# First attention: VectorE normalises an older group before, not after, the sixth row maximum of a pass

## The chip, the cores and the metric

The kernel runs on one core of a Trainium2 chip. The metric is the device time of one execution, in microseconds (us). The engines are named as in the profile: PE is TensorE (matmuls), PEld its loading of weights, DVE is VectorE, ACT is ScalarE, POOL is GpSimd and SP is SyncE, which issues the DMAs here. All run at once, each works through its own instructions in order, and they meet at semaphores.

## The reference

An input x of 4 sequences, 512 tokens each, 128 features, goes through two residual blocks. The change touches only the first, a causal attention of 16 heads with 8 features each:

```python
q = _gelu(apply_rope(x @ wqr + bqr));  k = _gelu(apply_rope(x @ wkr + bkr))
v = _gelu(x @ wkv + bkv) @ wv + bv
scores = einsum('bhqd,bhkd->bhqk', q, k) / sqrt(8), causal
attn = softmax(scores);  out = einsum('bhqk,bhkd->bhqd', attn, v) @ wo + bo
x = x + layernorm(that of layernorm(x));  x = x + layernorm(six layers of local attention and FFN)
```

The second block is six layers of windowed attention and gated FFN, and takes most of the time. Nothing of it is changed.

## The kernel before

**The first attention.** The 16 heads of each of the 4 sequences are cut into 4 groups of 4 heads, which gives 16 groups (`GROUPS`). A group goes through three passes of a software pipeline, so that pass i works on three groups at once: it finds the row maxima of group i, computes the exponentials of group i-1, and divides the outputs of group i-2 by their sums. Passes 0 to 17 run; each has 8 steps n = 0 to 7 (`A_STEPS`).

**One step.** PE scores two heads of group i, queries by keys (`score_for_max`, matmuls of L888), then scores two heads of group i-1 again, keys by queries with the maximum already subtracted (`score_for_exp`, L906), and then adds the causal mask to the first of these (`cut_later_keys`, L895). DVE takes the negated row maxima of the first (L676), ACT the exponentials of the second (L535), and POOL clears the masked corner (L480). The widths fall over the steps: 512 keys in steps 0 and 1, 128 in steps 6 and 7.

**What a pass has besides.** After step 4 (`OUT_AFTER`), PE turns the summed outputs of group i-2 into rows of tokens (`turn_out`, L934), and DVE's `normalise(i-2)` takes the reciprocal of the 16 sums of each token (L664) and multiplies (L666, into a_o, which lies in k_hat). DVE does that in step 5, behind that step's row maximum. At the end of a pass PE multiplies the exponentials with the values (`mix_heads`, L917), and between its parts turns the row maxima (`turn_max`, L926); DVE adds them to the queries (L682), and ACT copies the outputs (L540).

**The ring of PSUM slots.** All these results go through four PSUM slots (`a_ring`, two banks each), used in turn in the order of `a_plan`: in each step max, exp; after step 4 out; after step 7 turn. A user of a slot waits until the one four places earlier has been read (`wait_slot`). Around step 5 the order is: exp 3, max 4, exp 4, **out**, max 5, exp 5, max 6, **exp 6**, max 7, exp 7, turn. So exp 6 takes the slot of out and waits for `a_onorm`, which the multiply of `normalise` raises; max 7 takes the slot of max 5 and waits for its row maxima (`a_max`); the mixing and turn take the slot of max 6.

```python
                elif kind == "out":
                    pe.wait_ge(a_onorm.sem, a_onorm.done(group))
```

PE's own order in a step is fixed: max n, exp n, cut n; behind step 4 also `turn_out`. The heads' queries and keys come to their padded places by SP's DMAs (`move_heads(b)`, L393), those of sequences 2 and 3 after the last exponential scores of sequences 0 and 1.

Of the kernel before, what the change touches and what calls it, by code (L numbers as in the profile page):

```python
# [17 lines left out]
A_GROUPS, A_STEPS, A_ROW, OUT_AFTER = 4, 8, 9, 4  # L18
# [103 lines left out]
def sandwich_kernel(nc, x, wqr, bqr, wkv, bkv, wkr, bkr, wv, bv, wo, bo, w_qk, w_vt, w_o, qk_scale, w1, w2, ffn_vec,  # L122
                    c_ident, c_rope, c_causal, c_ones, c_band, c_sel, c_sel_rows, c_rot, out):
    ctx = ExitStack()
    with ctx:
# [221 lines left out]
        def ring(kind, group, n):  # L347

            at = a_plan.index((kind, group, n))
            return a_ring[at % len(a_ring)], a_plan[at - len(a_ring)] if at >= len(a_ring) else None  # L350

        def max_step(n):

            return TT - 1 - n // 2, n % 2
# [261 lines left out]
        def _(vector):  # L616
# [42 lines left out]
            def normalise(group):  # L659
                b, g = group // A_GROUPS, group % A_GROUPS  # L660
                slot, _ = ring("out", group, OUT_AFTER)
                o = slot[:, 0, :].rearrange("p (t j n) -> p t j n", t=TT, j=4)
                dve.wait_ge(a_oturned.sem, a_oturned.done(group))
                nc.vector.reciprocal(a_inv[:, :, :], o[:, :, :, A_HD]).then_inc(a_recip.sem, 1)  # L664
                dve.wait_ge(a_recip.sem, a_recip.done(group))
                nc.vector.tensor_tensor(a_o[:, b, :].rearrange("p (t j g d) -> p t j g d", t=TT, j=4, g=A_GROUPS)[:, :, :, g, :], o[:, :, :, 0:A_HD],  # L666
                                        a_inv[:, :, :].unsqueeze(3).to_broadcast([P, TT, 4, A_HD]), ALU.mult).then_inc(a_onorm.sem, 1)

            for i in range(GROUPS + 2):
                for n in range(A_STEPS):  # L670
                    if i < GROUPS:
                        qt, pair = max_step(n)
                        slot, _ = ring("max", i, n)
                        top_row = a_nmax[:, qt, :].rearrange("p (j n) -> p j n", j=4)[:, 2 * pair:2 * pair + 2, A_HD]
                        dve.wait_ge(a_scored.sem, a_scored.done(i, n))
                        nc.vector.tensor_reduce(top_row, slot[:, :, 0:P * (qt + 1)], AX.X, ALU.max, negate=True).then_inc(a_max.sem, 1)  # L676
                    if n == OUT_AFTER + 1 and i >= 2:
                        normalise(i - 2)
                if i < GROUPS:
                    slot, _ = ring("turn", i, 0)  # L680
                    dve.wait_ge(a_mturned.sem, a_mturned.done(i))
                    nc.vector.tensor_tensor(a_qaug[i % 2][:, :], a_qpad[:, 4 * (i // A_GROUPS % 2) + i % A_GROUPS, :], slot[:, 0, :], ALU.add).then_inc(a_aug.sem, 1)  # L682
# [535 lines left out]
```

## Time and profile before

| | |
|---|---|
| median of 3 runs | 2115.53 us (2112.12 to 2119.7) |
| span of the profiled execution | 2110.2 us |
| PE busy | 1875.9 us, 89% |
| DVE busy | 1560.5 us, 74% |
| ACT busy | 913.3 us, 43% |
| POOL busy | 1102.0 us, 52% |

The first attention's passes with both row maxima and normalising (2 to 15) lie between about 84 and 278 us of the span; the six layers between about 330 us and the end. Busy time is given for each engine by itself. PE's matmuls overlap one another, so that two rows with nearly the same start are matmuls running side by side on different rows of the array. The granted clock is what TensorE's throttle let through: 1.00 is 2.4 GHz, 0.50 is 1.2 GHz.

### The profile page before, as it was taken

The page shows a single profiled execution, that of the slowest core. Times are in us where ns is not written, and L with a number is a line of the kernel's source. Part 1 is how long each engine was busy: PE and PEld are TensorE (multiplying, and loading weights), DVE is VectorE, ACT ScalarE, POOL GpSimd, SP SyncE. Part 2 cuts the span into 40 slices and gives each one's busy share as a digit, 9 for nine tenths or more (in the row PEclk, how much of TensorE's full clock was granted, in tenths as well). Part 3 has the DMA queues.
Part 4 walks back from the last instruction along what each step waited for, and adds up shares of the span by engine and source line. Part 5 has one row for each costly group of instructions (what it writes and reads, how often), then busy time and mean ns, then how long its engine had stood idle before and what let it go on. Part 6 is the DMA issues. An engine that isn't in the chain of part 4 may idle for free.

```text
span 2110.2 us, 47076 instructions
## 1 busy us (share of the span) xinstructions
PE 1875.9 (89%) x20040; PEld 812.5 (39%) x20040; DVE 1560.5 (74%) x2524; ACT 913.3 (43%) x1460; POOL 1102.0 (52%) x822
## 2 busy tenths in 40 slices
PE   5999956799999999999999999999999998999974
PEld 2333423344334433444344344333443344344421
DVE  5555557877887788778877877888778878787823
ACT  1344422334454444445444544444444444544531
POOL 2122213765576557655755675567546755675520
PEclk9899987889999999999999999999999999999987
DMA  2200001121311132112212212131113211221100
GB/s 57 81 12 11 1 1 72 69 79 49 115 71 47 53 104 93 64 52 76 94 54 86 81 61 74 59 120 61 49 54 110 86 57 62 80 72 46 57 0 20
DMA packets 91750, 131.42 MB, mean 62 GB/s; under 512 B 16242, under 2 KB 35856, under 8 KB 91536
## 3 DMA queue, kind: packets, MB, share of 16 engines
q1 hardware_dynamic: 91540, 128.41, 17.6%
q8 instruction: 157, 2.57, 0.5%
q14 instruction: 53, 0.43, 0.1%
HBM read 24.54 MB, written 1.05 MB: 12 GB/s over the span
## 4 chain that ended last, share of the span: by engine, by line
PE 67%; DVE 21%; POOL 4%; issue 3%; ACT 2%; DMA 2%; SPq 0%; POOLq 0%; DVEq 0%; ACTq 0%
PE ps_z L1080 15%; PE ps_r L1003 11%; PE ps_s L1056 7%; DVE t L756 6%; PE ps_r L1110 4%; PE ps_z L1072 3%; PE ps_r L1117 3%; PE ps_r L1113 3%; PE ps_z L1013 2%; DVE t L676 2%; POOL k_hat L490 2%; DVE n_tmp L718 2%; PE ps_z L888 2%; DVE rnorm L723 2%; DVE n_tmp L720 2%
## 5 line engine op out<-in xcount | busy, mean ns | idle before, releaser
L756 DVE TENSOR_TENSOR t<-ps_r,rot 128x1024 f32<-128x1024 f32 x384 | 457.8, 1214 | 143.2 <-PE ps_r L1003 136.6
L1003 PE MATMUL ps_r<-xs,w_qk_sb 128*128 128x512 f32 x768 | 436.0, 673 | 41.0 <-ACT sq L556 40.5
L556 ACT ACTIVATE sq<-ps_r 128x512 f32<-128x512 f32 x384 | 229.6, 598 | 353.0 <-DVE t L756 350.7
L490 POOL TENSOR_TENSOR q_hat<-t 128x512 f32<-128x512 f32 x192 | 241.9, 1272 | 210.8 <-DMA t<-t 210.3
L1080 PE MATMUL ps_z<-z,vo 128*128 128x512 f32 x768 | 350.1, 599 | 0.0
L494 POOL TENSOR_TENSOR prob<-prob,top 128x1024 f32<-128x1024 f32 x96 | 182.5, 1901 | 280.2 <-DVE top L785 280.1
L490 POOL TENSOR_TENSOR k_hat<-t 128x512 f32<-128x512 f32 x192 | 242.3, 1276 | 86.4 <-DMA t<-t 86.3
L1003 PEld LDWEIGHTS ps_r<-xs,w_qk_sb 128*128 128x128 f32 x768 | 130.7, 200 | 293.9 <-ACT sq L556 173.4
L504 POOL TENSOR_TENSOR prob<-prob,sinv 128x1024 f32<-128x1024 f32 x96 | 185.9, 1936 | 90.5 <-DVE sinv L790 90.5
L578 ACT ACTIVATE z<-ps_z 128x512 f32<-128x512 f32 x384 | 208.1, 603 | 36.1 <-PE ps_z L1072 35.9
L1080 PEld LDWEIGHTS ps_z<-z,vo 128*128 128x128 f32 x768 | 144.6, 191 | 180.0 <-issue 179.9
L1072 PE MATMUL ps_z<-pt,xtk 32*128 32x512 f32 x1536 | 196.9, 628 | 7.8 <-ACT z L578 6.5
L500 POOL TENSOR_TENSOR prob<-prob,rnorm 128x1024 f32<-128x1024 f32 x96 | 182.6, 1902 | 7.5 <-POOL prob L494 0.4
L480 POOL TENSOR_SCALAR_AFFINE_SELECT t<-t 128x256 f32<-128x256 f32 x128 | 51.9, 406 | 217.8 <-ACT t L535 217.6
L1056 PE MATMUL ps_s<-k_hat,q_hat 64*32 64x64 f32 x12288 | 151.5, 228 | 14.3 <-DVE prob L781 7.8
L1056 PEld LDWEIGHTS ps_s<-k_hat,q_hat 64*32 64x32 f32 x12288 | 131.2, 106 | 75.4 <-DVE prob L781 43.6
L781 DVE TENSOR_TENSOR prob<-ps_s,band 128x1024 f32<-128x1024 f32 x96 | 117.1, 1220 | 54.5 <-PE ps_s L1056 54.4
L777 DVE TENSOR_TENSOR k_hat<-k_hat,ps_s 128x1024 f32<-128x1024 f32 x96 | 116.5, 1213 | 30.6 <-PE ps_s L1037 30.6
L608 ACT ACTIVATE gate<-ps_r,vec 128x512 f32<-128x512 f32 (+1 forms) x72 | 49.4, 685 | 206.1 <-PE ps_r L1110 205.8
L788 DVE TENSOR_REDUCE sinv<-prob 128x16 f32<-128x1024 f32 x96 | 116.1, 1209 | 10.6 <-ACT prob L573 10.6
L794 DVE STREAM_TRANSPOSE pt<-prob 128x1024 f32<-128x1024 f32 x96 | 117.4, 1223 | 8.1 <-POOL prob L504 4.6
L1072 PEld LDWEIGHTS ps_z<-pt,xtk 32*128 32x128 f32 x1536 | 70.5, 187 | 127.2 <-ACT z L578 58.8
(188 smaller groups left out, 2560.4 us busy)
## 6 DMA issues: line engine op xcount, KB each, us to landing
t<-t SPq DMA_DIRECT2D x768, 128.0 KB, 2.0
rot<-in_dram SPq DMA_DIRECT2D x12, 512.0 KB, 4.8
w_qk_sb<-in_dram SPq DMA_DIRECT2D x24, 256.0 KB, 3.3
w_vt_sb<-in_dram SPq DMA_DIRECT2D x6, 512.0 KB, 4.7
w_o_sb<-in_dram SPq DMA_DIRECT2D x6, 512.0 KB, 5.8
z<-q_hat SPq DMA_DIRECT2D x128, 16.0 KB
w_sb<-in_dram SPq DMA_DIRECT2D x6, 341.0 KB
x_tok<-in_dram SPq DMA_DIRECT2D x4, 256.0 KB, 3.6
```

Of the source, the lines that this page charges most:

```text
L490: nc.gpsimd.tensor_tensor(dst, t12[:, slot, 0, :], t2[:, slot, :], ALU.add).then_inc(added.sem, 1)
L494: nc.gpsimd.tensor_tensor(s, s, top[:, (TT * u + n) % P_SLOTS, :].unsqueeze(2).to_broadcast([P, HEADS, 2 * WIN]), ALU.subtract).then_inc(l ...
L500: nc.gpsimd.tensor_tensor(s, s, by.unsqueeze(2).to_broadcast([P, HEADS, 2 * WIN]), ALU.mult).then_inc(scaled.sem, 1)
L504: nc.gpsimd.tensor_tensor(s, s, sinv[:, (TT * u + n) % P_SLOTS, :].unsqueeze(2).to_broadcast([P, HEADS, 2 * WIN]), ALU.mult).then_inc(p_no ...
L556: nc.scalar.activation(sq[:, n % SQ_SLOTS, :], ps_r[n % 2][:, :], ACT.Square).then_inc(squared.sem, 1)
L578: nc.scalar.activation(z[:, :, at:at + WIN], ps_z[:, w, :].rearrange("p (h n) -> p h n", n=WIN), ACT.Copy).then_inc(z_copied.sem, 1)
L756: nc.vector.tensor_tensor(t12[:, slot, :, :], ps_r[n % 2][:, :].unsqueeze(1).to_broadcast([P, 2, SEQ]), rot[:, n // PAIRS, :, :], ALU.mult ...
L794: nc.vector.transpose(pt[:, n % 2, :, :, :].rearrange("p h a n -> p (h a n)"), prob[:, (TT * u + n) % P_SLOTS, :, :, :].rearrange("p c e n ...
L1003: nc.tensor.matmul(ps_r[n % 2][:, :], w_qk_sb[:, n, :], xs[:, seq, WIN:WIN + SEQ], start=True, stop=True).then_inc(projected.sem, 1)
L1056: ins = nc.tensor.matmul(ps_s[WIN * w:WIN * (w + 1), e, 2 * WIN * c:2 * WIN * (c + 1)], q_hat[rows, pair_at(c), at:at + WIN], k_hat[rows, ...
L1072: ins = nc.tensor.matmul(ps_z[:, w, :], xtk[rows, a, n, :], pt[rows, n % 2, :, a, :], start=(a == 0), stop=(a == 1), skip_group_check=True)
L1080: ins = nc.tensor.matmul(ps_z[:, 0, :], vo[:, h, :], z[:, h, :], start=(h == 0), stop=False, skip_group_check=True)
```

## The change

In DVE's order, `normalise(i - 2)` moves from behind the row maximum of step 5 to ahead of it. It is still behind that of step 4. No instruction is added or taken away, none changes its operands, and the orders of the other engines are as they were.

```diff
             for i in range(GROUPS + 2):
                 for n in range(A_STEPS):
+                    if n == OUT_AFTER + 1 and i >= 2:
+                        normalise(i - 2)
                     if i < GROUPS:
                         qt, pair = max_step(n)
...
                         dve.wait_ge(a_scored.sem, a_scored.done(i, n))
                         nc.vector.tensor_reduce(top_row, slot[:, :, 0:P * (qt + 1)], AX.X, ALU.max, negate=True).then_inc(a_max.sem, 1)
-                    if n == OUT_AFTER + 1 and i >= 2:
-                        normalise(i - 2)
```

## Rows read from the trace of the kernel before

**Rows 1.** The page: the span, and the clock granted to PE in 40 slices.
```profile
span 2110.2 us, 47076 instructions
...
PEclk9899987889999999999999999999999999999987
```

**Rows 2.** Windows: stretch, length, busy us (instructions) of each engine, clock, DMA share, GB/s.
```profile
84.00:278.00 194.00, 176.96 (x1704) 77.47 (x1692) 106.72 (x155) 87.14 (x126) 45.52 (x112) 0.96 0.06 14
330.00:2110.00 1780.00, 1620.50 (x17965) 695.56 (x17963) 1381.21 (x2155) 799.18 (x1293) 1029.67 (x674) 0.96 0.20 69
```

**Rows 3.** Who waited for the multiply of normalise: total us, times.
```profile
  PE ps_s L906: 6.0, 7
  PE ps_z L906: 6.0, 7
```

**Rows 4.** Timeline, pass 8: start, duration, engine, line, operation, [idle before <-releaser].
```profile
172.15 0.66 PE L934 MATMUL ps_s<-ident,t 128*128 128x128 f32 x4 [0.19 <-DVE t L676]
173.38 0.28 PE L895 MATMUL ps_r<-causal_bf,ident_bf 128*128 128x128 bf16 x2
173.51 0.60 ACT L535 ACTIVATE t<-ps_z 128x512 f32<-128x512 f32 x1 [1.11 <-PE ps_z L906]
173.60 0.49 PE L888 MATMUL ps_z<-z 32*128 32x128 f32 x4
173.70 0.69 DVE L676 TENSOR_REDUCE t<-ps_r 128x2 f32<-128x512 f32 x1 [1.01 <-PE ps_r L895]
174.31 0.25 DVE L664 RECIPROCAL a_inv<-ps_s 128x16 f32<-128x16 f32 x1
174.59 0.29 DVE L666 TENSOR_TENSOR k_hat<-ps_s,a_inv 128x128 f32<-128x128 f32 x1
174.94 0.49 PE L906 MATMUL ps_s<-xsq,z 32*128 32x128 f32 x4 [0.85 <-DVE k_hat L666]
175.58 0.38 PE L888 MATMUL ps_r<-z 32*128 32x128 f32 x2
176.23 1.06 PE L917 MATMUL ps_z<-t,sq 128*32 128x512 f32 x8
```

**Rows 5.** Timeline, pass 1, which has no normalising: steps 5 to 7.
```profile
80.22 0.28 PE L895 MATMUL ps_z<-causal_bf,ident_bf 128*128 128x128 bf16 x2
80.43 0.38 PE L888 MATMUL ps_r<-z 32*128 32x128 f32 x2
80.54 0.69 DVE L676 TENSOR_REDUCE t<-ps_z 128x2 f32<-128x512 f32 x1 [0.43 <-PE ps_z L895]
81.28 0.38 PE L888 MATMUL ps_z<-z 32*128 32x128 f32 x2
81.94 1.06 PE L917 MATMUL ps_r<-t,sq 128*32 128x512 f32 x8
```

**Rows 6.** Timeline, pass 16, where DVE has no row maxima to take.
```profile
281.21 0.66 PE L934 MATMUL ps_z<-ident,t 128*128 128x128 f32 x4 [0.21 <-ACT t L535]
281.91 0.26 DVE L664 RECIPROCAL a_inv<-ps_z 128x16 f32<-128x16 f32 x1 [4.50 <-PE ps_z L934]
```

**Rows 7.** Timeline of DVE: additions at the ends of passes 1, 2 and 15.
```profile
83.63 0.69 DVE L682 TENSOR_TENSOR xsq<-z,ps_r 128x512 f32<-128x512 f32 x1 [1.16 <-PE ps_r L926]
96.89 0.69 DVE L682 TENSOR_TENSOR xc<-z,ps_z 128x512 f32<-128x512 f32 x1 [1.16 <-PE ps_z L926]
...
276.72 0.69 DVE L682 TENSOR_TENSOR xsq<-z,ps_r 128x512 f32<-128x512 f32 x1 [1.16 <-PE ps_r L926]
```

**Rows 8.** Windows of PE alone (length, busy us, clock), at the first and the last of four falls.
```profile
146.00:147.00 1.00, 0.15 (x4) 1.00 0.00 0
147.00:148.00 1.00, 1.00 (x10) 0.59 0.00 0
...
259.00:260.00 1.00, 1.00 (x14) 0.91 0.00 0
```

**Rows 9.** Timeline: SP's DMAs that move sequence 3's heads.
```profile
176.18 21.62 SPq L393 DMA_DIRECT2D z<-q_hat  x32
```

## The prediction

> **What bounds the kernel now.** I read the page first: a span of 2110.2 us, TensorE at full clock in most slices [rows 1]. The change lies in one stage, passes 2 to 15 of the first attention, 84 to 278 us of it, so nothing can be read off the shares of the whole. In that stage PE is busy 177.0 of 194 us [rows 2]: it leads, but with gaps. The table of waits, asked for the multiply of normalise, names one gap that belongs to this change: PE's exponential scores (L906) sat idle for it 7 + 7 = 14 times, 12.0 us in all, 0.86 us each [rows 3]. Fourteen is the number of passes from 2 to 15, so it happens in each.
>
> The timeline of pass 8 shows how [rows 4]. PE turns the older group's outputs at 172.15; they are ready at 172.81. DVE has ended the maximum of step 4 by 172.69 (173.70 less the 1.01 in its row) and then stands idle, since the next thing in its order, the maximum of step 5, needs scores whose mask is added only at 173.38. It runs from 173.70, and only behind it come the reciprocal (174.31) and the multiply (174.59 to 174.88). PE, at step 6 since 173.60, gets its max scores away, but its exponential scores want the slot that the multiply reads, and start at 174.94. DVE thus idles with a job in hand that PE later waits for.
>
> **The change, part by part.** Two DVE instructions in each of 14 passes go ahead of one. They add no work, have no DMA with them, and DVE issues nothing else there; SP's and POOL's queues are not passed. In passes 16 and 17 there is no maximum to pass, so the order there stays as it was.
>
> *Where the normalising lands.* What it newly shows, a wait of the reciprocal for PE's turning, is bounded by pass 16, where DVE does wait for just that: the reciprocal starts 281.91 - 281.21 = 0.70 us behind the start of the turning [rows 6]. In pass 8 that is 172.15 + 0.70 = 172.85. The multiply starts 0.28 later (174.59 - 174.31) at 173.13 and ends 0.29 later at 173.42 [rows 4]. Behind the waiting reciprocal stands the maximum of step 5, which starts at 173.70; it is covered by 0.28 us. So this move costs nothing; if the cover were gone, each 0.1 us beyond it would cost 14 x 0.1 = 1.4 us, because that maximum frees a slot on the path, as follows.
>
> *What PE gets.* PE took 0.06 us from the multiply's end (174.88) to its scores (174.94) [rows 4]; after 173.42 that makes 173.48, ahead of the 173.60 at which PE comes to step 6. The wait goes altogether, by a margin of 0.12 us, and the two scores of step 6 run side by side.
>
> *What is late next.* Max 7 needs the slot of max 5, whose maximum ends at 173.70 + 0.69 = 174.39. Pass 1 shows this order with nothing else in it, because it has no older group: its maximum of step 5 runs from 80.54 to 81.23, and step 7 starts at 81.28, 0.05 behind it, 0.85 behind step 6 (80.43) [rows 5]. So in pass 8 step 7 starts at 173.60 + 0.85 = 174.45 instead of 175.58: 1.13 us earlier. The check by the other ends agrees: from the mask of step 5 to the first mixing, pass 1 takes 81.94 - 80.22 = 1.72 us and pass 8 takes 176.23 - 173.38 = 2.85 us, a difference of 1.13 [rows 4, 5]. The bounds of this term: 0.85, if only the wait as recorded goes [rows 4], and 1.34, the distance from 173.60 to 174.94, if the new wait for maximum 5 cost nothing either. I take 1.13, since pass 1 is the same code at the same clock.
>
> The later end of the pass follows PE: mixing, turning, addition and ACT's copy all keep their distances from it, and an unhindered pass would take 13.26 (96.89 - 83.63 [rows 7]) - 1.13 = 12.13 us. POOL is busy 45.5 and ACT 87.1 of 194 us [rows 2], so neither becomes the bound. SP moves sequence 3's heads from 176.18 for 21.62 us [rows 9], behind pass 8, and pass 12 needs them: the three passes between, of 12.13 each, are 36.4 us, so they stay hidden.
>
> Sum of this part: 14 x 1.13 = 15.8 us (bounds 14 x 0.85 = 11.9 and 14 x 1.34 = 18.8).
>
> *The clock.* From the end of pass 1 to that of pass 15 go 276.72 - 83.63 = 193.09 us, and 14 x 13.26 would be 185.64: 7.45 us are lost elsewhere. The windows show how: in four of these passes the granted clock falls from 1.00 to 0.50 for some microseconds, and PE's work takes longer there. Each fall starts within a microsecond behind the 0.85 us wait. The first: the clock is at 1.00 in 146 to 147, where PE was busy 0.15 us, and 0.59 in the microsecond after; the last begins in 259 to 260 [rows 8]. None starts elsewhere in these passes. With the wait gone, PE works through what is now a hole, and its longest remaining ones are the 0.19 us ahead of the turning [rows 4] and about as much ahead of step 7 (0.85 less the 0.65 that such a step takes, 176.23 - 175.58 [rows 4]). So I expect these falls to go; the bounds are 0 and 7.45 us, and I take 7.45, since all four stand behind this wait and ten passes without a fall had just the same work.
>
> Against it speaks the Trainium skill: its page "TensorE: Matmul & The Clock Gate", section "HAM oscillation", has the clock fall for much longer pauses than the one here. The same page, "A second HAM failure mode", tells of short pauses between groups of matmuls that made the clock swing. The trace agrees with the second, as four falls behind waits of 0.85 us show; by the first alone the falls would have another cause and stay, which is the second rival's case.
>
> **The sum.** 15.8 + 7.5 = 23.3 us. The profiled execution would come to 2110.2 - 23.3 = 2086.9. The median of the runs is 5.3 above that execution's span, and I keep this distance: 2115.5 - 23.3 = 2092.2 us.
>
> **The rivals.**
> 1. *The falls stay, or come elsewhere in the stage.* A pass is as full of narrow matmuls as before, and the granted clock was also low elsewhere. Then only the first part is earned: 2115.5 - 15.8 = 2099.7. For it: the falls come in only 4 of 14 passes, so the wait alone doesn't decide. Against it: their place.
> 2. *The margins don't hold.* 0.12 us for the exponential scores and 0.28 for the maximum are small. If the normalising came half a microsecond late, maximum 5 and with it step 7 would be 0.22 late in each pass: 14 x 0.22 = 3.1 less gain; with the falls gone 2095.3, with them staying 2102.8.
> 3. *The change doesn't do what it says.* If the exponential scores of step 6 in truth waited for something that ended along with the multiply, such as ACT's reading of a slot, the wait would stay and the time with it: 2115.5. The rows name the multiply 14 times out of 14, and ACT's exponentials of step 5 end at 173.51 + 0.60 = 174.11, well before 174.94 [rows 3, 4], so I give this little.
> 4. *Slower.* The shift moves the six layers against whatever decides their falls; there the clock averages 0.96 over 1780 us, up to 0.04 x 1780 = 71 us at half clock [rows 2]. A fall cost 7.45 / 4 = 1.9 us in the first attention. To eat up the gain and 6.3 us more would take 29.6 / 1.9, some 16 further falls. From 13 on (23.3 / 1.9) nothing of the gain is left. Nothing in the order of that stage changes, so this is the tail.
>
> **How the numbers follow.** Forecast 0.56; rival 1 0.26; rival 2 0.09; rival 3 0.05; rival 4 0.04. The predicted time is the forecast's, 2092.2. The three runs spread from 3.4 below to 4.2 above their median. The range takes the forecast less 5 (spread, and a per-pass gain nearer to its upper bound) and rival 1 and both cases of rival 2 with most of their spread: 2087 to 2103. About 0.3%, 6.3 us, is what a measurement of this kernel can tell from no change. Faster by more than that are the forecast and rivals 1 and 2, all but a sliver: 0.90. Within it: rival 3 and that sliver, 0.06. Slower: 0.04.
>
> **What would show it.** Right: no wait of L906 for L666 in passes 2 to 15; a reciprocal that follows the turning (L934) by 0.70 us; step 7 starting 0.85 behind step 6, with a new short wait for L676; additions (L682) 12.13 us apart; no clock below 1.00 between pass 2 and pass 15; the six layers as long as before. Wrong: L906 still idle in step 6 with another releaser (rival 3); additions evenly 12.3 to 12.4 apart (rival 2); single passes of 13 to 15 us (rival 1); a longer stretch from the first attention's end to the end of the span (rival 4).

## The result, and the profile after

The changed kernel took 2081.88 us in the median of its 4 runs, against 2115.64 us for the kernel before. One of the 4, at 3491.93 us, was a disturbed execution, as was one of the kernel before beside e13 (2659.22 us), and the medians count these two while all ratios and ranges leave them out. The ratio is 0.9838, with a 95% interval of 0.98 to 0.9876, so the change is worth 26 to 42 us. Two later comparisons of the same pair gave 0.9852 (0.9824 to 0.9879) and 0.9864 (0.9834 to 0.9894). The forecast was a gain of 23.3 us and a time of 2092.2 us, with a range of 2087 to 2103. The direction was right and the range missed: the gain is larger than forecast.

The page of the profiled execution of the changed kernel gives the span, the busy times and the granted clock in 40 slices:

```profile
span 2082.9 us, 47076 instructions
...
PE 1854.6 (89%) x20040; PEld 804.1 (39%) x20040; DVE 1562.6 (75%) x2524; ACT 914.1 (44%) x1460; POOL 1101.8 (53%) x822
...
PEclk9899968999999999999999999999999999999987
```

DVE, ACT and POOL are as busy as before. PE is busy 21.3 us less with the same instructions, because the two kinds of scores of step 6 again run side by side, and because fewer matmuls run at half clock. The span is 27.3 us shorter. The timeline of pass 7 of the changed kernel (start, duration, engine, line, operation, idle time before) shows the rows that answer to [rows 4]. The row maxima are line 678 here:

```profile
151.91 0.66 PE L934 MATMUL ps_z<-ident,t 128*128 128x128 f32 x4 [0.19 <-DVE t L678]
...
152.60 0.26 DVE L664 RECIPROCAL a_inv<-ps_z 128x16 f32<-128x16 f32 x1
...
152.90 0.29 DVE L666 TENSOR_TENSOR k_hat<-ps_z,a_inv 128x128 f32<-128x128 f32 x1
...
153.14 0.29 PE L895 MATMUL ps_z<-causal_bf,ident_bf 128*128 128x128 bf16 x2
...
153.36 0.38 PE L888 MATMUL ps_r<-z 32*128 32x128 f32 x2
153.37 0.38 PE L906 MATMUL ps_z<-xc,z 32*128 32x128 f32 x2
...
153.47 0.69 DVE L678 TENSOR_REDUCE t<-ps_z 128x2 f32<-128x512 f32 x1 [0.28 <-PE ps_z L895]
...
154.21 0.19 PEld L888 LDWEIGHTS ps_z<-z 32*128 32x128 f32 x2 [0.31 <-DVE t L678]
154.21 0.38 PE L888 MATMUL ps_z<-z 32*128 32x128 f32 x2
...
154.86 1.06 PE L917 MATMUL ps_r<-t,sq 128*32 128x512 f32 x8
```

The reciprocal follows the turning by 0.69 us, and the row maximum of step 5 still finds DVE free (0.28 us idle before it). The exponential scores of step 6 start 0.01 behind its max scores, where they were 1.34 behind. Step 7 now waits for the row maxima of step 5 and starts 0.85 behind step 6. From the mask of step 5 to the mixing it is 154.86 - 153.14 = 1.72 us, as in pass 1 [rows 5], against 2.85 [rows 4].

The additions at the ends of passes answer to [rows 7]; here are those of passes 1, 2 and 15, on DVE:

```profile
83.76 0.69 DVE L682 TENSOR_TENSOR xsq<-z,ps_r 128x512 f32<-128x512 f32 x1 [1.16 <-PE ps_r L926]
...
95.89 0.69 DVE L682 TENSOR_TENSOR xc<-z,ps_z 128x512 f32<-128x512 f32 x1 [1.16 <-PE ps_z L926]
...
253.62 0.69 DVE L682 TENSOR_TENSOR xsq<-z,ps_r 128x512 f32<-128x512 f32 x1 [1.16 <-PE ps_r L926]
```

A pass takes 12.13 us, and 14 of them 169.86 = 14 x 12.13: none is longer than the others. Windows of the two kernels by stage (length, busy us and instructions of PE, PEld, DVE, ACT and POOL, granted clock, DMA share, GB/s), first before, then after:

```profile
84.00:278.00 194.00, 176.96 (x1704) 77.47 (x1692) 106.72 (x155) 87.14 (x126) 45.52 (x112) 0.96 0.06 14
278.00:334.60 56.60, 25.40 (x175) 17.98 (x169) 29.62 (x117) 10.03 (x17) 9.54 (x12) 0.67 0.00 1
334.60:2110.20 1775.60, 1615.90 (x17937) 691.19 (x17936) 1381.21 (x2155) 797.39 (x1290) 1029.67 (x674) 0.96 0.20 69
```

```profile
84.00:254.00 170.00, 163.02 (x1688) 71.22 (x1684) 107.30 (x155) 87.13 (x126) 45.51 (x112) 1.00 0.07 15
254.00:311.40 57.40, 26.23 (x193) 18.40 (x181) 29.90 (x118) 10.15 (x17) 9.59 (x12) 0.67 0.00 1
311.40:2082.90 1771.50, 1607.93 (x17937) 688.72 (x17936) 1382.53 (x2155) 798.04 (x1290) 1029.41 (x674) 0.96 0.20 69
```

So 23.2 of this pair's 27.3 us lie in passes 2 to 15 (193.09 - 169.86), as forecast (23.3), at a clock of 1.00 where it was 0.96, and 4.1 in the six layers, where nothing was forecast. That 23.2 meets 23.3 so closely is no test of the size of the clock term, because its 7.45 us were read from this same execution of the kernel before. What this pair doesn't explain is the difference of the medians, above 30 us. The experiments are about that, and about whether the forecast's two terms had the causes it named.

### The profile page after: what moved, and what is told of

It reads as the page before. It is cut to its first block, busy times and chain, and to the rows that moved or that the text cites. A ratio compares the mean times of both kernels' runs of the same rounds, so it can differ in the third digit from the quotient of the medians.

```text
span 2082.9 us, 47076 instructions
## 1 busy us (share of the span) xinstructions
PE 1854.6 (89%) x20040; PEld 804.1 (39%) x20040; DVE 1562.6 (75%) x2524; ACT 914.1 (44%) x1460; POOL 1101.8 (53%) x822
## 4 chain that ended last, share of the span: by engine, by line
PE 66%; DVE 20%; POOL 5%; issue 3%; ACT 2%; DMA 2%; SPq 0%; POOLq 0%; DVEq 0%; ACTq 0%
PE ps_z L1080 15%; PE ps_r L1003 11%; PE ps_s L1056 7%; DVE t L756 6%; PE ps_r L1110 4%; PE ps_r L1117 3%; PE ps_z L1072 3%; PE ps_r L1113 3%; POOL k_hat L490 2%; PE ps_z L1013 2%; DVE t L678 2%; DVE n_tmp L718 2%; PE ps_z L888 2%; DMA t<-t 2%; DVE rnorm L723 2%
## 5 line engine op out<-in xcount | busy, mean ns | idle before, releaser
L1056 PE MATMUL ps_s<-k_hat,q_hat 64*32 64x64 f32 x12288 | 151.7, 228 | 15.8 <-DVE prob L781 7.8
```

Source lines behind the costliest of these rows:

```text
L1056: ins = nc.tensor.matmul(ps_s[WIN * w:WIN * (w + 1), e, 2 * WIN * c:2 * WIN * (c + 1)], q_hat[rows, pair_at(c), at:at + WIN], k_hat[rows, ...
```

## Experiments

In what follows, "the stretch" is the time from the addition at the end of pass 1 to that of pass 15. A long pass is one of its 14 that takes over 14 us; the others of a kernel, which agree within 0.02 us, are its even passes. Each run has one profiled execution, from which stretches and passes are read; its time is the median of its executions.

**More runs of the changed kernel (e1).** No edit.

> The changed kernel as it is, for more runs of it beside more runs of the kernel before. The profiled pair differs by 27.3 us of span, of which 23.2 lie between the additions at the ends of passes 1 and 15 (193.09 against 169.86) and 4.1 behind them, while the medians of the runs differ by some 34 to 36 us. Theory A (the gain is that of the first attention alone, and the rest is chance in the layers' clock falls): the difference of the medians comes down to 23 to 28 us, ratio 0.987 to 0.989. Theory B (the layers are faster too, by a lasting amount): it stays at 33 to 37 us, ratio 0.9825 to 0.9845.

Measured: 2080.72 us (6 runs) against 2113.44 (17 runs), 32.7 us between the medians; ratio 0.9852 (0.9824 to 0.9879), which is 31 us. The ratio lies between the two theories' ranges and its interval reaches into both. In its profile the stretch is 169.87 us.

**The layers started as late as before (e2).** DVE repeats a copy that is made anyway, 32 times (from the edit):

```diff
+                for k in range(32 if b == 0 else 0):
+                    dve.wait_ge(padded.sem, k)
+                    nc.vector.tensor_copy(xs[0:64, b, WIN:WIN + SEQ], ps_t[b % 2][0:64, :]).then_inc(padded.sem, 1)
```

> The changed kernel with 32 idle copies of DVE (0.69 us each by the copies at this place, some 0.72 with the wait between them, 23 us in all) between the first attention and the six layers, so that the layers start about when they start in the kernel before. Everything is computed as in the changed kernel. Theory B1 (the layers' clock falls depend on when they start, and the change moved them to a better time): the further 11 us go, and the time is that of the kernel before, within 3 us (ratio 0.999 to 1.001). Theory B2 (the layers gain whatever their start): the time is that of the changed kernel plus 23 us, some 2103 (ratio 0.994 to 0.996).

Measured: 2107.15 us (12 runs), ratio 0.9966 (0.9942 to 0.9991). The copies took

```profile
299.89 22.90 DVE L701 COPY xs<-ps_z 64x512 f32<-64x512 f32 x32
```

It is 26.4 us above e1, where 22.9 were put in, and 6.3 below the kernel before. That is nearer to theory B2 (some 2103, 0.994 to 0.996) than to B1 (0.999 to 1.001), and the interval holds nearly all of B2's range and only the edge of B1's. The layers didn't simply fall back to the length that they have before.

**One layer instead of six (e3, e4).** Both kernels with `DEPTH = 1`; the other five layers are left out.

> The kernel before with one layer of the six (the other five are left out, so the output is another one). With e4 it gives the gain with little of the layers behind it. About 2110 less 5 layers of some 283 us (4 units of 70.9): some 690 us.

> The changed kernel with one layer of the six (five left out). Both theories: the first attention's 23.2 us (14 passes of 1.13 and 7.4 of clock falls) less than e3. Theory A and B1: e3 less 21 to 26 us. Theory B2, if the lasting gain sits in what is common to all layers: about a sixth of 11 us more, 25 us; if it sits at the handing over from the first attention: 34 us less than e3.

Measured: 699.43 (694.35 to 703.37) and 669.44 us (666.59 to 670.98), a difference of 30.0 us, above the 21 to 26 that the 23.2 us would leave room for and below the 34. (The 690 us reckoned for e3 were 9 too few.) The profiles say where a part of it lies. The additions of passes 1 and 15 of e3 are

```profile
83.17 0.69 DVE L682 TENSOR_TENSOR xsq<-z,ps_r 128x512 f32<-128x512 f32 x1 [1.16 <-PE ps_r L926]
...
279.86 0.69 DVE L682 TENSOR_TENSOR xsq<-z,ps_r 128x512 f32<-128x512 f32 x1 [2.49 <-PE ps_r L926]
```

With the old order the stretch was 279.86 - 83.17 = 196.69 us, with the new one 250.86 - 81.00 = 169.86. The new order takes the same time as in the changed kernel; the old one took 3.6 us more than in the page before. That gave the next question.

**The old order, profiled again (e5, e6).** No edit to the kernel before.

> The kernel before as it is, for a second look at its first attention (the one layer kernel showed 196.69 us between the additions of passes 1 and 15 where the page before shows 193.09; the changed order gave 169.86 in each of four looks). Theory C (the profile of before on which the prediction rests was one with few clock falls; its other executions lose more there): the stretch takes 195 to 203 us here, with 6 to 9 falls. Theory D (the attention's gain is 23 to 27 us in all runs, and the rest is in the layers): 191 to 197 us.

> The kernel before once more, as e5: theory C 195 to 203 us for that stretch, theory D 191 to 197 us. The six layers (from their first projection to the end) 1770 to 1780 us by both.

Measured: 2115.89 and 2109.85 us. The stretch was 193.13 and 199.73 us. The additions of passes 1 and 15 of e6:

```profile
83.69 0.69 DVE L682 TENSOR_TENSOR xsq<-z,ps_r 128x512 f32<-128x512 f32 x1 [1.16 <-PE ps_r L926]
...
283.42 0.69 DVE L682 TENSOR_TENSOR xsq<-z,ps_r 128x512 f32<-128x512 f32 x1 [2.49 <-PE ps_r L926]
```

So four profiled executions of the old order (before, e3, e5, e6) gave 193.09, 196.69, 193.13 and 199.73 us, a mean of 195.7, with 4, 6, 4 and 7 long passes (14.7 to 15.7 us); all others are 13.26. e5 lies in theory D's range and below C's, e6 in C's alone; its six layers took 1767.5 us, where both theories had 1770 to 1780. C is right in that the execution behind the prediction was a low one, but not by as much as I had set down for every execution, and e5 is as low, with its long passes in the same places (6, 10, 13 and 14). In all 21 falls of the four, the clock leaves 1.00 within 0.9 us behind the end of a 0.85 us wait; but 35 of the 56 waits have no fall behind them. In eight profiled executions of the new order (after, e1, e2, e4, e13 to e16) the stretch was 169.85 to 169.87 us each time. The first attention's gain is 195.7 - 169.9 = 25.8 us on average: 14 x 1.13 = 15.8 from the order and 10.0 from the clock. With four executions of the old order that mean is rough: single ones give 23.2 to 29.9.

**The same hole filled, in the old order (e10).** DVE's order is that of the kernel before; PE makes the max scores of step 6 three times over in the passes that have a normalising, the same values in the same place (from the edit):

```diff
-                for e in range(2):
+                for e in [0, 1] * (3 if n == OUT_AFTER + 2 and group >= 2 else 1):
```

> The kernel before, DVE's old order, but PE makes the two max scores of step 6 three times over in passes 2 to 15 (the same values into the same place, 0.43 us a time), which fills its hole of 0.85 us with work that nobody needs. Theory F: no falls, while the passes stay 13.26 apart (up to 13.35): the stretch is 185.6 to 187 us, and the time falls to about 2104, the 25.8 us of the changed kernel less 15.8. If also the further 7 us of difference between the medians came with the falls, 2097. Theory G: falls as before, 193 to 200 us, 2114.

Measured: 2102.03 us (6 runs) against 2116.57 (11 runs), ratio 0.9943 (0.992 to 0.9965). The timeline of step 6 in it:

```profile
159.95 0.25 DVE L664 RECIPROCAL a_inv<-ps_z 128x16 f32<-128x16 f32 x1
160.23 0.29 DVE L666 TENSOR_TENSOR k_hat<-ps_z,a_inv 128x128 f32<-128x128 f32 x1
160.58 0.49 PE L906 MATMUL ps_z<-xc,z 32*128 32x128 f32 x4 [0.40 <-DVE k_hat L666]
```

and its window over passes 2 to 15, beside that of e6 in the next fence (columns as above):

```profile
84.00:270.00 186.00, 175.27 (x1800) 81.59 (x1804) 106.82 (x155) 87.22 (x126) 45.72 (x112) 1.00 0.07 16
```

```profile
84.00:285.00 201.00, 183.97 (x1692) 79.48 (x1688) 106.79 (x155) 87.15 (x126) 45.51 (x112) 0.92 0.06 15
```

The fill took less time than reckoned, and a hole of 0.40 us was left of the 0.85. That was enough, as the additions of passes 1 and 15 show:

```profile
84.02 0.69 DVE L682 TENSOR_TENSOR xsq<-z,ps_r 128x512 f32<-128x512 f32 x1 [1.16 <-PE ps_r L926]
...
269.61 0.69 DVE L682 TENSOR_TENSOR xsq<-z,ps_r 128x512 f32<-128x512 f32 x1 [1.16 <-PE ps_r L926]
```

There is not one long pass, and the stretch is 269.61 - 84.02 = 185.59 us, which is 14 x 13.26, at a clock of 1.00. PE does more work, each pass is as long as before, and the kernel is some 12 us faster (7 to 17 by the interval), as theory F had it. This shows the second term of the forecast by itself: the clock fell because PE stood idle there. DVE's order and the length of a pass are those of the kernel before, so neither of these brings the falls by itself.

**The hole put back into the new order (e7, e8, e9).** DVE adds 128x512 (and, in e9, one 128x128 more) into a place that is not read, ahead of the normalising of each pass. This is e7's edit, with its neighbouring lines:

```diff
                     if n == OUT_AFTER + 1 and i >= 2:
+                        for k in range(1):
+                            dve.wait_ge(spun.sem, 1 * (i - 2) + k)
+                            nc.vector.tensor_tensor(gate[:, 0, :], gate[:, 1, :], gate[:, 1, :], ALU.add).then_inc(spun.sem, 1)
                         normalise(i - 2)
```

> The changed kernel with one further DVE addition of 128x512 (0.69 us, written to a place that is not read) ahead of the normalising of each pass. It ends at 173.95 instead of 173.42 in the times of pass 8, so the exponential scores of step 6 come 0.41 late and the row maxima of step 5 0.25 late. Theory of the ring (step 7 waits for the row maxima of step 5): 0.25 us a pass, additions 12.38 apart, 3.5 us in all. Theory that the exponential scores alone set the pass: 0.41 and 12.54. Clock: with a hole of 0.4 us, fewer falls than in the kernel before, 0 to 2.

> The same with two such additions, 1.38 us. The exponential scores of step 6 come 1.1 late and the row maxima of step 5 0.94 late: additions 13.06 to 13.1 apart, 13 us more than in the changed kernel without falls. Here PE has again a hole of about 0.9 us at the place of the one removed, while DVE's order is the new one. Theory F (the hole is what lets the clock fall): 3 to 8 falls in passes 2 to 15, each right behind the hole. Theory G (the falls came from the old order in some other way): none, and 14 equal passes.

> As e8, with a third addition of 128x128 (0.29 us by the multiply of that shape) behind the two of 128x512. In e8 the hole of PE in step 6 was 0.61 us and no fall came in 14 passes; here it is 0.9 us, as in the kernel before (0.85), with DVE's order still the new one. Additions 13.01 + 0.29 = 13.30 apart where the clock holds. Theory F (the width of the hole lets the clock fall): 3 to 7 falls in passes 2 to 15, each within a microsecond behind the hole, passes of 14.7 and more, the stretch of 14 passes 193 to 201 us. Theory G (the old order in some other way): no fall, 186 us.

Measured in the stretch: e7 172.02 us (passes of 12.29, no long one), e8 182.18 us (13.01, none), e9 203.68 us (even passes 13.34, eight others from 14.0 to 16.0). The table of waits says how long PE's scores of step 6 waited for the multiply, in e8 and in e9 (total us, times, longest):

```profile
PE ps_s L910 <- DVE k_hat L667: 4.3, 7, 0.6
PE ps_z L910 <- DVE k_hat L667: 4.2, 7, 0.6
```

```profile
PE ps_s L911 <- DVE k_hat L667: 6.8, 7, 1.2
PE ps_z L911 <- DVE k_hat L667: 6.5, 7, 0.9
```

And their windows over these passes, e8 first:

```profile
84.00:266.00 182.00, 168.43 (x1684) 75.00 (x1676) 125.14 (x183) 87.22 (x126) 45.69 (x112) 1.00 0.07 15
```

```profile
84.00:288.00 204.00, 185.61 (x1688) 80.44 (x1684) 129.76 (x197) 87.23 (x126) 47.68 (x112) 0.91 0.06 13
```

In e8 the hole was 0.61 us, where I had reckoned with 0.9, and the clock was left alone in 14 passes: taken by itself, that is what theory G had forecast. Holes of 0.93 us in e9 brought the falls back, with the new order of DVE: eight, one more than I had set down, in a stretch longer than the 193 to 201 us expected, and one of them 2.0 us behind its hole. That speaks for the hole and against theory G. In e7 no fall came either, as expected. In e7 a pass is 0.16 us longer than without the addition, nearer to the ring's 0.25 than to the 0.41 of the other theory; DVE's instructions follow each other more closely than I had reckoned. The times of these three are single runs, 2100.07, 2095.64 and 2132.85 us. That of e7 is far above what its stretch would give (2.2 us above the changed kernel's), because its six layers took 1786.3 us in that run. More on that below.

**Two steps of order further (e11), and the turning moved (e12).** In e11 the normalising goes ahead of the row maxima of step 4 (`if n == OUT_AFTER and i >= 2:`). In e12 `OUT_AFTER` is 5, which moves the turning behind step 5 and the normalising ahead of the maxima of step 6.

> The changed kernel with the normalising still one place earlier, ahead of the row maxima of step 4. It waits there for PE's turning, and the row maxima of step 4 behind it with it: in the times of pass 8 they start at 173.42 instead of 172.01 and end at 174.10, and PE's exponential scores of step 5 want their slot: 174.16 instead of 172.75, 1.4 us late in each pass, less 0.1 to 0.4 that the shorter way behind it gives back. Additions 13.1 to 13.6 apart, 14 to 20 us slower than the changed kernel, and again falls of the clock. If PE's queue hid it: 12.13 apart.

> The changed kernel with the turning of the outputs and the normalising one step later (behind step 5, the normalising ahead of the row maxima of step 6). The turning no longer waits 0.19 us for the row maxima of step 3, and the step behind it has the time. Step 7 then waits for the normalising: at 174.33 instead of 174.45 in the times of pass 8: additions 12.0 apart, 1.5 us gain in all, too little for the medians. If the row maxima of step 3 hold step 5 instead: 12.1 to 12.3, no gain.

Measured: e11 2117.07 us in one run, stretch 204.35 us, even passes 13.46 and eight long ones. Its waits of PE:

```profile
PE ps_z L906 <- DVE t L678: 4.5, 7, 0.6
PE ps_s L906 <- DVE t L678: 4.5, 7, 0.6
```

The gain is gone: in this kernel a place too early costs as much as one too late. The passes lie in the range expected (13.1 to 13.6), and the falls came too. Here holes of 0.64 us, in step 5, go along with eight long passes, where 0.61 us in step 6 (e8) went with none. The two differ in more than the place: over a whole even pass, PE is idle 13.46 - 12.32 = 1.14 us in e11 and 13.01 - 12.04 = 0.97 in e8. So the width of one hole is not a rule that can be carried over, and which of the differences counts was not tested.

e12: 2079.8 us (4 runs, 2072.71 to 2088.8), ratio 0.9829 (0.9789 to 0.9869), not to be told from the changed kernel. Its passes are 12.18 us, 0.05 longer than the changed kernel's, which is the second of the two outcomes set down (12.1 to 12.3, no gain). The turning no longer waits, but the max scores of step 5 do:

```profile
PE ps_z L888 <- DVE t L678: 1.3, 7, 0.2
PE ps_s L888 <- DVE t L678: 1.3, 7, 0.2
```

The wait for the row maxima of step 3 only changed hands. No better version came of it.

**What the last microseconds are (e13 to e16).** The changed kernel again, and with 1, 2 and 3 of e2's copies.

> The changed kernel as it is, the base for e14 to e16: 2080 to 2083, ratio to before 0.983 to 0.986.

> The changed kernel with 1 idle copy (0.72 us) between the first attention and the layers. Theory P (the layers' length hangs on when they start): the medians of e13 to e16, each less its copies, differ by 4 us or more. Theory N (it doesn't; what is left is chance): they agree within 2.5 us, here 2081 to 2084.

> 2 idle copies (1.43 us). Theory P: some 4 us or more off e13 plus 1.4, in either direction. Theory N: 2082 to 2085.

> 3 idle copies (2.15 us). Theory P: as e15, another distance. Theory N: 2082 to 2085.

Measured, medians of 6 runs each: 2084.77 (2080 to 2083 expected), 2089.52, 2084.51 and 2087.31 us. Less their copies: 2084.8, 2088.8, 2083.1 and 2085.2. They differ by up to 5.7 us, which by the letter is what theory P had forecast (4 or more). But within each kernel the six runs differ by 8 to 13 us, and the changed kernel itself differs by 4.1 us between e1 and e13. So this doesn't decide between P and N. What it does show is the size of the chance: a difference of 5 us between medians of six runs is not worth an explanation here. Against the kernel before, e13 is at 0.9864 (0.9834 to 0.9894), 22 to 35 us, and 25.8 lies in that.

## Why the prediction was wrong in size and right in kind

**The reading of the stage** held in each number that the timeline of the changed kernel gives: the reciprocal 0.69 us behind the turning (0.70 forecast), the row maximum of step 5 not delayed (0.28 us of cover forecast, 0.28 measured), the scores of step 6 side by side, step 7 behind by 0.85. A pass takes 12.13 us, as forecast. The term of 14 x 1.13 = 15.8 us is right; pass 1, the same code without the older group, was the row that fixed it.

**The clock term** had the right cause (e10 without the hole, e9 with it) and the wrong size. I took 7.45 us from one execution and made the same 7.45 its upper bound. Four executions of the old order lose 7.5, 11.1, 7.5 and 14.1 us (each stretch less 185.6), 10.0 on average. The one that I had was the lowest of the four, by 0.04 us. A loss that comes in 4 of 14 passes varies from one execution to the next, and one execution gives no bound for it. This alone doesn't explain the miss: with 10.0 in place of 7.45 the forecast would have been 2115.5 - 25.8 = 2089.7 us, inside the range.

**The carrying over to the median** is the step that took the time out of the range. I let one profiled execution stand for the median, with nothing for the layers and a constant 5.3 us between span and median. The measured 2081.88 us lies 10.3 below the forecast, and the same pair shows where. The layers took 4.1 us less, where I had put nothing. And the median lies 1.0 us below the new profiled span (2081.88 against 2082.9), where I had put it 5.3 above, which is another 6.3. How much of this lasts is the open question below. Of the 5.3 only 1.7 to 1.9 lie around the span (2084.59 - 2082.9 in the profiled run of the changed kernel; 2115.89 - 2114.2 in e5; 2112.12, the lowest run, if it is the profiled one, less 2110.2). The rest is the difference between one execution and another. Part of that can be clock falls that the change takes away too, and I treated it as something that stays. The spread of the runs doesn't settle how much: 45 executions of the old order lie between 2104.2 and 2127.0 us, 15 of the changed kernel between 2076.4 and 2091.3.

**The rivals.** The first (falls stay) is refuted in eight profiled executions. The second (margins) and the third (no effect) are refuted by the timeline above. The fourth (more falls in the layers) didn't come: the layers, from their first projection to the end, took 1771.6, 1770.7 and 1771.6 us in the profiled executions of after, e1 and e13, and 1775.6, 1778.8 and 1767.5 in before, e5 and e6. Its sum was wrong, though without weight in the forecast: a mean clock of 0.96 over 1780 us means 0.08 x 1780 = 142 us at half clock, of which half, 71 us, is lost. The clock fell behind holes of 0.85 us, and with 0.40 left of them it didn't (e10). The Trainium skill has, on its page "TensorE: Matmul & The Clock Gate", section "HAM oscillation", the clock fall for much longer pauses. The prediction set this beside the case that the falls stay, which is its first rival and not, as it says there, its second. The trace decides against that rule as the reason for these falls. The same page of the Trainium skill, in "A second HAM failure mode", tells of frequent short pauses between groups of matmuls; that is the passage that this kernel bears out.

**What stays open.** With 25.8 us in the first attention, the measured 34, 31 and 29 us leave 8, 5 and 3 over. Some of that can be the roughness of the 25.8 itself. Three profiled executions of each kernel (before, e5, e6; after, e1, e13) differ by 30.2 us in the mean of their spans (2110.8 and 2080.6): 25.4 in the stretch, 1.1 before it, 0.9 between the first attention and the layers, 2.7 in the layers. The code before the stretch is the same, so I take that 1.1 for chance. The layers' times go from 1767.5 to 1786.3 us over the profiled executions of all kernels with six layers, so 2.7 can be chance as well. A lasting gain of a few us in the layers isn't shown, nor is it excluded; e2, e14, e15 and e16 didn't settle it.

## What to carry to other kernels

When an engine stands idle in its order with a finished input at hand while another engine waits for what it would make of it, put that work into the idle time, and look for the place from both sides: here one place later cost 1.13 us a pass, one place earlier 1.33. A pass of the same loop in which the moved work doesn't exist gave the size of this move to 0.01 us. A short hole of TensorE can cost more than its length: behind the 0.85 us holes here the clock fell in 4 to 7 of 14 passes, 7.5 to 14.1 us in all. That part varies from run to run, so profile several executions before giving it a size and a bound, and don't let one profiled execution stand for the median.

## What was not expected of the hardware

Two repetitions of a score that nobody needs, in each of 14 passes, made the kernel faster: 2102.03 against 2116.57 us, without shortening a single even pass. They took half of what I had put them at (0.43 us each): 0.40 of the 0.85 us stayed idle. And the width of a hole alone doesn't seem to tell whether the clock falls: 0.61 us in step 6 gave no fall in 14 passes, 0.64 us in step 5 gave eight, each in one profiled execution.
